# The last feed forward of a decoder: a pipeline over pairs of items, candidates split at the eighth key

## The chip, the cores and the metric

One core of one Trainium2 chip runs the whole kernel in one launch. The metric is the device time of that core in microseconds (us), as the median of several runs; less is better. The engines of a core work side by side and meet only at semaphores: TensorE (PE, with its weight loads PEld), VectorE (DVE), ScalarE (ACT), GpSimd (POOL) and SyncE (SP).

## What is computed

A decoder of four layers on x of 32 items x 128 tokens x 128 features, in float32; each layer has an attention, a cross attention and a feed forward. Only the last of these twelve stages is touched. For each item it computes, of the normalised x (`hidden_states`):

```python
H=4 heads, nk=64 keys, K=8, 512 experts
sim = einsum('pbthn,hkpn->pbthk', q, keys)          # q = hidden_states @ W_q.T, p = x half and y half
scores_xy, idx_xy = top_k(sim, K)                   # the 8 best keys of each half
all_scores = sx[..., :, None] + sy[..., None, :]    # 64 sums per head
all_idx = ix[..., :, None] * nk + iy[..., None, :]
scores, pk = top_k(all_scores, K)                   # the 8 best sums
w = silu(hidden . down_embed[indices] * softmax(scores))
experts_states = sum over h, k of w * up_embed[indices]
dense = silu(hidden @ W_up.T) @ W_down.T
x = x + dense + experts_states
```

There are 512 embeddings, and an index is ix * 64 + iy. So an index whose x key is 8 or more lies past the end and is taken as the last one, 511. Both kernels use this: only the first 8 x keys need a grid of 8 x 64 = 512 weights, one per embedding, and what falls on all other x keys goes to embedding 511.

## The kernel before, in words

Tokens lie on the 128 partitions. The stage is `l3_ffn`, with 32 items in a hardware loop of 16 trips of U = 2 items on each engine (`Fori`, lines 2563, 2630 and 2653). Inside a trip every engine goes through its steps for item 0 and item 1, and each step waits on a semaphore with the item's number. Nothing of the next trip begins before the last step of this one: VectorE's first step (L100, normalise) comes after its last (L2626, x plus result).

The order within a trip, per item:

- VectorE normalises; TensorE transposes (L2656) and ScalarE copies to xT (L2633); TensorE multiplies by W_q (L2660), ScalarE copies to qT (L2636); TensorE multiplies by down_embed (L2663, 128x512, into `p_dot`) and by the keys (L2666, into `p_sim`), then by W_up (L2670).
- VectorE takes the 8 best of each half and head (L2573), finds the places of the x ones (L2576), builds 64 candidate sums per head (L2582) and 512 grid sums per head (L2586), and takes the 8 best candidates (L2593).
- ScalarE takes exp of all 2304 sums (L2639). VectorE zeroes what is under the eighth best (L2599, L2602), adds up and inverts (L2605, L2606), and multiplies by the inverse and by `p_dot` (L2609, L2611). ScalarE takes silu of 2304 (L2645).
- VectorE sums what fell past the eighth key (L2616, L2618, L2620) and adds the four heads (L2622, L2623). TensorE transposes the 512 weights (L2675), ScalarE copies (L2648), TensorE multiplies the dense and the expert parts into `p_dot` (L2681, L2683), VectorE adds to x (L2626).

The helper `skewed` (L180), used by other stages and by the changed one, yields steps t: the step calls `item(lag)` and gets pair t - lag, if there is one. The first steps stand as straight code, then a loop, then straight code again. `Steps` is the `Chain` of the other stages; a chained instruction is waited for on its own engine.

## Time and profile before

| | us |
|---|---|
| median of 3 runs | 6312.41 (6308.8 to 6314.84) |
| the profiled execution, own time | 6316.28 |
| its span | 6314.5 |
| VectorE busy in it | 3620.7 (57%) |
| TensorE busy | 3596.9 (57%) |
| ScalarE busy | 1577.1 (25%) |
| last stage in it, first instruction to last | 5531.2 to 6304.2 |

Reading: the page gives whole-span shares, which mix twelve stages. The last stage is the stretch from 5531 us on, and its rows come from the views by stretch. A row of the groups by line says: line, engine, operation, tiles written <- read, shapes, xcount | busy us, mean ns of one | idle time before it and who ended it. A row of the timeline says: start us, duration, engine, line, operation, xcount, and in brackets the idle time before it and who ended that. Neighbouring instructions on an engine overlap, so the distance between starts can be less than the duration; the chain of work gives that distance. In a row of the windows the stretch and its length come first, then the busy time and count of PE, PEld, DVE, ACT and POOL, then the granted TensorE clock (1.00 is 2.4 GHz, 0.50 is 1.2 GHz), the DMA share and GB/s. A float32 matmul shows as two instructions (x8 is 4 of them).

### The profile page before, as it was taken

What the parts mean: (1) busy time and instruction counts of PE and PEld (TensorE: products, weight loads), DVE (VectorE), ACT (ScalarE), POOL (GpSimd) and SP (SyncE); (2) the same over time, 40 slices, a digit from 0 to 9 for tenths busy, and PEclk for the clock granted to TensorE, in tenths of its full rate; (3) what the DMA queues carried; (4) which work ended last, traced back from release to release, by engine and by line L of the source; (5) the groups of instructions that cost most, each with busy time, mean ns of one, the idle gap of its engine ahead of it and who ended that gap; (6) DMA issues with size and microseconds to landing.
All of it is one profiled execution on the core that took longest, in us unless ns stands there. A gap on an engine that the chain in (4) does not pass through costs nothing. (4 is left out here: it accounts for less than half of the span.)

```text
span 6314.5 us, 71361 instructions
## 1 busy us (share of the span) xinstructions
PE 3596.9 (57%) x21570; PEld 2472.5 (39%) x21634; DVE 3620.7 (57%) x10096; ACT 1577.1 (25%) x3714; POOL 749.3 (12%) x1030
## 2 busy tenths in 40 slices
PE   4679999534346601601533344489978887833333
PEld 4456666312114400501422233356656665523222
DVE  2453333688896530554577755444446665567776
ACT  1452232100004300200111111233324443423332
POOL 0240000000003257075000000000000000000000
PEclk9789999766668755555655556589989999966666
DMA  3000000000000000300200000000000000000000
GB/s 80 4 10 5 10 10 5 8 0 0 0 0 12 16 2 1 84 1 3 59 0 0 0 6 0 7 3 10 7 14 0 0 0 3 0 10 0 0 0 13
DMA packets 84128, 60.48 MB, mean 10 GB/s; under 512 B 21067, under 2 KB 78744, under 8 KB 83332
## 3 DMA queue, kind: packets, MB, share of 16 engines
q1 hardware_dynamic: 67164, 56.87, 3.2%
q0 software_dynamic: 12288, 0.68, 0.2%
q10 hardware_dynamic: 4608, 2.10, 0.1%
q8 instruction: 34, 0.56, 0.0%
q14 instruction: 34, 0.28, 0.0%
HBM read 64.98 MB, written 19.14 MB: 13 GB/s over the span
## 5 line engine op out<-in xcount | busy, mean ns | idle before, releaser
L398 DVE TENSOR_TENSOR l_ffn_h<-l_ffn_sg,l_ffn_p_u 128x512 f32<-128x512 f32 (+1 forms) x448 | 308.0, 688 | 408.2 <-PE l_ffn_p_u L371 406.6
L387 ACT ACTIVATE l_ffn_sg<-l_ffn_p_g 128x512 f32<-128x512 f32 (+1 forms) x448 | 267.5, 597 | 819.0 <-PE l_ffn_p_g L368 805.0
L371 PE MATMUL l_ffn_p_u<-l_ffn_f_xTall,l_ffn_wu 128*128 (+1 forms) x896 | 461.2, 596 | 8.4 <-DVE l_ffn_h L398 8.4
L368 PE MATMUL l_ffn_p_g<-l_ffn_f_xTall,l_ffn_wg 128*128 (+1 forms) x896 | 461.8, 597 | 1.9 <-DVE l_ffn_f_logits L259 1.0
L377 PEld LDWEIGHTS l_ffn_p_o<-l_ffn_wd,l_ffn_h 128*128 128x128 f32 (+1 forms) x3584 | 410.3, 192 | 31.0 <-issue 31.0
L377 PE MATMUL l_ffn_p_o<-l_ffn_wd,l_ffn_h 128*128 128x128 f32 (+1 forms) x3584 | 410.6, 275 | 0.0
L95 POOL TENSOR_TENSOR rstd<-vareps,minus_half 128x32 f32<-128x32 f32 x12 | 65.2, 5435 | 2860.9 <-DVE vareps L86 2134.2
L994 PE MATMUL l_attn_p_s<-l_attn_outer,l_attn_upper 128*128 128x512 f32 x256 | 191.7, 917 | 298.5 <-DVE l_attn_outer L905 232.0
L407 DVE SCALAR_TENSOR_TENSOR x<-l_ffn_p_o,l_ffn_cw,x 128x128 f32 x512 | 171.2, 351 | 284.2 <-PE l_ffn_p_o L377 282.4
L2675 PE MATMUL l_ffn_p_sim<-ident,l_ffn_w 128*128 128x128 f32 x128 | 35.6, 433 | 481.8 <-DVE l_ffn_w L2623 481.8
L371 PEld LDWEIGHTS l_ffn_p_u<-l_ffn_f_xTall,l_ffn_wu 128*128 128x128 f32 (+1 forms) x896 | 166.2, 186 | 230.5 <-issue 221.3
L368 PEld LDWEIGHTS l_ffn_p_g<-l_ffn_f_xTall,l_ffn_wg 128*128 128x128 f32 (+1 forms) x896 | 162.2, 186 | 192.2 <-issue 191.7
L994 PEld LDWEIGHTS l_attn_p_s<-l_attn_outer,l_attn_upper 128*128 128x128 f32 x256 | 73.5, 302 | 412.2 <-issue 331.6
L2281 ACT ACTIVATE l_attn_E<-l_attn_p_s,l_attn_nm 128x128 f32<-128x128 f32 x512 | 182.7, 382 | 156.3 <-DVE l_attn_nm L2244 156.3
L1641 POOL DMA_INDIRECT l_combine_got<-slots_out,l_combine_at x192 | 211.0, 1099 | 60.7 <-issue 49.0
L2675 PEld LDWEIGHTS l_ffn_p_sim<-ident,l_ffn_w 128*128 128x128 f32 x128 | 22.8, 216 | 491.2 <-DVE l_ffn_w L2623 491.2
L1745 PE MATMUL l_attn_p_t<-ident,l_attn_xhat 128*128 128x128 f32 x32 | 9.6, 448 | 340.8 <-DVE l_attn_xhat L100 340.8
L1426 POOL DMA_INDIRECT slots_in<-l_route_xd,l_route_at x192 | 187.3, 975 | 58.1 <-issue 40.5
L1936 PE MATMUL l_film_p_a<-ident,l_film_mean 128*120 128x128 f32 x32 | 15.0, 467 | 306.9 <-DVE l_film_mean L1873 306.9
L371 PE MATMUL l_route_p_u<-l_route_f_xTall,l_route_wu 128*88 x32 | 19.5, 696 | 263.4 <-issue 263.4
L980 ACT ACTIVATE l_attn_st<-l_attn_st 128x32 f32<-128x32 f32 x48 | 11.0, 229 | 603.6 <-DVE l_attn_st L885 333.7
L2301 PEld LDWEIGHTS l_attn_p_y<-l_attn_xT,l_attn_wqkv 128*128 128x128 f32 x1024 | 130.2, 192 | 42.7 <-issue 31.5
(690 smaller groups left out, 8992.1 us busy)
## 6 DMA issues: line engine op xcount, KB each, us to landing
l_attn_toep<-kernel_rows SPq DMA_DIRECT2D x1, 8192.0 KB, 31.5
ssm_toep<-ssm_rows SPq DMA_DIRECT2D x1, 8192.0 KB, 31.4
l_slots_w<-in_L_ffn_w SPq DMA_DIRECT2D x32, 176.0 KB, 2.3
slots_in<-l_route_xd,l_route_at POOLq DMA_INDIRECT x192
l_combine_got<-slots_out,l_combine_at POOLq DMA_INDIRECT x192
l_slots_w<-in_L_ffn_w SPq DMA_DIRECT2D x32, 88.0 KB
x<-in_x SPq DMA_DIRECT2D x1, 2048.0 KB
l_ffn_wg<-in_L_ffn_w_gate SPq DMA_DIRECT2D x8, 256.0 KB, 2.7
```

Source lines behind the costliest of these rows:

```text
L95: pool.tensor_tensor(R.rstd[:], R.vareps[:], R.minus_half[:], ALU.pow).then_inc(s.rstd_ready, 1)
L368: pe.matmul(X.p_g[0:X.FP, k % 2], X.wg[:, w, f * X.FP:(f + 1) * X.FP], x, start=True, stop=True).then_inc(s.gate_psum, 1)
L371: pe.matmul(X.p_u[0:X.FP, k % 2], X.wu[:, w, f * X.FP:(f + 1) * X.FP], x, start=True, stop=True).then_inc(s.up_psum, 1)
L377: mm = pe.matmul(X.p_o[:, v, q * P:(q + 1) * P], X.h[:, v, f, q * P:(q + 1) * P], X.wd[:, w, f * P:(f + 1) * P], start=(f == 0), stop=(f = ...
L387: act.activation(X.sg[:, k % 2], X.p_g[0:X.FP, k % 2], ACT.Silu).then_inc(s.silu_ready, 1)
L398: dve.tensor_tensor(X.h[:, k // X.FC, k % X.FC], X.sg[:, k % 2], X.p_u[0:X.FP, k % 2], ALU.mult).then_inc(s.h_ready, 1)
L407: add = dve.scalar_tensor_tensor(out=row(R.x, b), in0=X.p_o[:, v, q * P:(q + 1) * P], scalar=weight, in1=row(R.x, b), op0=ALU.mult, op1=AL ...
L994: mm = pe.matmul(p_s[:, r, a], upper[:], outer[:, u, r, a * 512:(a + 1) * 512], start=True, stop=True)
L1426: pool.indirect_dma_start(xb, bass.IndirectOffsetOnAxis(ap=at[:, u, k:k + 1], axis=0), xd[:, u], None, bounds_check=last, oob_is_err=False ...
L1641: pool.indirect_dma_start(got[:, u, k], None, yb, bass.IndirectOffsetOnAxis(ap=at[:, u, k:k + 1], axis=0), bounds_check=last, oob_is_err=F ...
L2281: e = act.activation(E[:, u % 2, h], p_s[:, u % 2, odd, c * P:(c + 1) * P], ACT.Exp, bias=nm[:, u % 2, h:h + 1], accum_out=sums[:, u % 2, ...
L2301: mm = pe.matmul(p_y[:, c * P:(c + 1) * P], wqkv[:, w:w + P], xT[:, u // 2], start=True, stop=True)
```

## The change

The stage works on pairs (16) as a pipeline of depth 3: in step t, pair t is normalised and scored (item 0), pair t-1 gets its candidates, sums and exp (item 1), pair t-2 its weights (item 2), and pair t-3 is transposed, multiplied and added to x (item 3). There are 19 steps. The x keys are split at the eighth: the 16 x values per head are the first 8 keys and the 8 best of the other 56, so no place has to be looked up, and `cand` holds 128 sums per head. VectorE multiplies exp by `p_dot` and by the comparison with the eighth best, while the division is left to ScalarE: silu gets the inverse as its per-partition `scale`, one activation per head, and a second, with an accumulator, sums what goes to embedding 511. The four heads are added by TensorE: 16 matmuls with the identity per item, accumulating in PSUM, stand in place of 4 transposes. x comes to the output sum by a matmul with the identity; ScalarE copies the result back over x, and normalises too. Lines that stand for removed or unchanged code are "...".

```diff
@@ -2525,23 +2525,23 @@
...
+    NG_, NC = H * NE, H * 2 * K * K
+    W, PAIRS, PER2 = 2 * P, NB // 2, 2
+    with phase(nc, "l3_ffn", "var_ready rstd_ready shift_ready w_in vchain xhat_ready xT_psum xT_ready q_psum q_ready sim_psum sums_ready cut_ready exp_ready "
+                   "dot_psum w_ready silu_ready rest_added up_psum h_ready wT_psum wT_ready out_psum out_taken") as (s, sb, ps):
...
+        xhat, xT, qT = sb("xhat", [P, W]), sb("xT", [P, PER2, W]), sb("qT", [P, HF, W])
+        top, first, m, xs = sb("top", [P, 2, 2 * H, K]), sb("first", [P, 2 * H]), sb("m", [P, 2 * H]), sb("xs", [P, 2 * H, 2 * K])
+        sums, cand = sb("sums", [P, PER2, 2, NG_]), sb("cand", [P, PER2, 2 * H, 2 * K * K])
+        cut, fit, z = sb("cut", [P, PER2, 2 * H, K]), sb("fit", [P, 2 * H, K * K]), sb("z", [P, 2 * H])
+        w, e_c, e_t = sb("w", [P, PER2, 2, NG_]), sb("e_c", [P, PER2, 2 * H, K * K]), sb("e_t", [P, PER2, 2 * H, K])
+        rz, rest, spare = sb("rz", [P, PER2, 2 * H]), sb("rest", [P, PER2, 2 * H]), sb("spare", [P, K * K])
+        hT, wT = sb("hT", [P, PER2, HF, W]), sb("wT", [P, 2, HF, P])
+        p_q, p_sim, p_dot = ps("p_q", [P, HF, W]), ps("p_sim", [P, 2, 512]), ps("p_dot", [P, 2, 512])
+        p_w, p_x = ps("p_w", [P, 512]), ps("p_x", [P, 2, W])
...
@@ -2554,134 +2554,160 @@
...
+                chain = Steps(dve, s.vchain)
...
+                def added(b, u, r):
+                    dve.wait_ge(s.silu_ready, b * 2 + (r + 1))
+                    last = w[:, u, r].rearrange("p (h k) -> p h k", h=H)[:, :, NE - 1]
+                    dve.tensor_tensor(last, last, rest[:, u, r * H:(r + 1) * H], ALU.add).then_inc(s.rest_added, 1)
+                for item in skewed(dve, 3, PAIRS, PER2):
...
+                    for b, u in item(3):
+                        added(b, u, 0)
+                    for b, u in item(1):
+                        sim = p_sim[:].rearrange("p r (a h k) -> p r a h k", a=2, h=H)
+                        dve.wait_ge(s.sim_psum, b * 2 + 2)
+                        dve.tensor_reduce(first[:].rearrange("p (r h) -> p r h", r=2), sim[:, :, 0, :, 0:K], AX.X, ALU.max)
+                        for r in range(2):
...
+                                dve.max(top[:, 0, r * H + h], sim[:, r, 0, h, K:NK])
+                                last = dve.max(top[:, 1, r * H + h], sim[:, r, 1, h])
...
+                        chain(dve.tensor_tensor(m[:], first[:], top[:, 0, :, 0], ALU.max))
+                        chain(dve.tensor_tensor(m[:], m[:], top[:, 1, :, 0], ALU.add))
+                        dve.tensor_tensor(xs[:, :, 0:K].rearrange("p (r h) k -> p r h k", r=2), sim[:, :, 0, :, 0:K],
+                                          m[:].rearrange("p (r h) -> p r h", r=2).unsqueeze(3).broadcast_to((P, 2, H, K)), ALU.subtract)
+                        chain(dve.tensor_tensor(xs[:, :, K:2 * K], top[:, 0], m[:].unsqueeze(2).broadcast_to((P, 2 * H, K)), ALU.subtract))
+                        chain(dve.tensor_tensor(cand[:, u].rearrange("p g (i j) -> p g i j", i=2 * K),
+                                                xs[:].unsqueeze(3).broadcast_to((P, 2 * H, 2 * K, K)),
+                                                top[:, 1].unsqueeze(2).broadcast_to((P, 2 * H, 2 * K, K)), ALU.add))
+                        for g in range(2 * H):
+                            last = dve.max(cut[:, u, g], cand[:, u, g])
+                        last.then_inc(s.cut_ready, 1)
+                    for b, u in item(3):
+                        added(b, u, 1)
+                    for b, u in item(1):
+                        for r in range(2):
+                            dve.tensor_tensor(sums[:, u, r].rearrange("p (h i j) -> p h i j", h=H, i=K),
+                                              xs[:, r * H:(r + 1) * H, 0:K].unsqueeze(3).broadcast_to((P, H, K, NK)),
+                                              sim[:, r, 1].unsqueeze(2).broadcast_to((P, H, K, NK)), ALU.add).then_inc(s.sums_ready, 1)
+                    for b, u in item(2):
+                        dve.wait_ge(s.exp_ready, b + 1)
+                        chain(dve.tensor_reduce(z[:], e_t[:, u], AX.X, ALU.add))
+                        dve.reciprocal(rz[:, u], z[:])
+                        chain(dve.tensor_tensor(fit[:], cand[:, u, :, K * K:2 * K * K], cut[:, u, :, K - 1:K].broadcast_to((P, 2 * H, K * K)), ALU.is_ge))
+                        for r in range(2):
+                            dve.wait_ge(s.dot_psum, b * 2 + (r + 1))
+                            chain(dve.tensor_tensor(w[:, u, r].rearrange("p (h k) -> p h k", h=H), w[:, u, r].rearrange("p (h k) -> p h k", h=H),
+                                                    p_dot[:, r].unsqueeze(1).broadcast_to((P, H, NE)), ALU.mult))
+                            g = slice(r * H, (r + 1) * H)
+                            dve.scalar_tensor_tensor(out=e_c[:, u, g].rearrange("p g k -> p (g k)"), in0=e_c[:, u, g].rearrange("p g k -> p (g k)"),
+                                                     scalar=p_dot[:, r, NE - 1:NE], in1=fit[:, g].rearrange("p g k -> p (g k)"), op0=ALU.mult, op1=ALU.mult)
+                            for h in range(H):
+                                n = slice(h * NE, (h + 1) * NE)
+                                last = dve.scalar_tensor_tensor(out=w[:, u, r, n], in0=sums[:, u, r, n], scalar=cut[:, u, r * H + h, K - 1:K],
+                                                                in1=w[:, u, r, n], op0=ALU.is_ge, op1=ALU.mult)
+                            last.then_inc(s.w_ready, 1)
...
+                def silus(b, u, r):
+                    act.wait_ge(s.w_ready, b * 2 + (r + 1))
+                    for h in range(H):
+                        n, g = slice(h * NE, (h + 1) * NE), r * H + h
+                        act.activation(w[:, u, r, n], w[:, u, r, n], ACT.Silu, scale=rz[:, u, g:g + 1])
+                        last = act.activation(e_c[:, u, g], e_c[:, u, g], ACT.Silu, scale=rz[:, u, g:g + 1], accum_out=rest[:, u, g:g + 1])
+                    last.then_inc(s.silu_ready, 1)
+                act.wait_ge(s.shift_ready, 1)
+                for item in skewed(act, 3, PAIRS, PER2):
+                    for b, u in item(3):
+                        silus(b, u, 1)
+                    for b, u in item(2):
+                        act.wait_ge(s.up_psum, b + 1)
+                        act.activation(hT[:, u].rearrange("p c t -> p (c t)"), p_q[:].rearrange("p c t -> p (c t)"), ACT.Silu).then_inc(s.h_ready, 1)
+                    for b, u in item(0):
+                        for r in range(2):
+                            last = act.activation(xhat[:, r * P:(r + 1) * P], row(R.x, b * 2 + r), ACT.Identity,
+                                                  scale=R.rstd[:, bass.ds(b * 2 + r, 1)], bias=R.shift[:, bass.ds(b * 2 + r, 1)])
+                        last.then_inc(s.xhat_ready, 1)
+                    for b, u in item(3):
+                        for r in range(2):
+                            act.wait_ge(s.wT_psum, b * 2 + (r + 1))
+                            act.activation(wT[:, r].rearrange("p c t -> p (c t)"), p_w[:], ACT.Copy).then_inc(s.wT_ready, 1)
+                        act.wait_ge(s.out_psum, b + 1)
+                        act.activation(pair(R.x, b), side(p_x[:, 1]), ACT.Copy).then_inc(s.out_taken, 1)
+                    for b, u in item(0):
+                        act.wait_ge(s.xT_psum, b + 1)
+                        act.activation(xT[:, u], p_x[:, 0], ACT.Copy).then_inc(s.xT_ready, 1)
+                        act.wait_ge(s.q_psum, b + 1)
+                        act.activation(qT[:].rearrange("p c t -> p (c t)"), p_q[:].rearrange("p c t -> p (c t)"), ACT.Copy).then_inc(s.q_ready, 1)
+                    for b, u in item(1):
+                        act.wait_ge(s.cut_ready, b + 1)
+                        act.activation(e_c[:, u], cand[:, u, :, K * K:2 * K * K], ACT.Exp)
+                        act.activation(e_t[:, u].rearrange("p g k -> p (g k)"), cut[:, u].rearrange("p g k -> p (g k)"), ACT.Exp)
+                        for r in range(2):
+                            act.wait_ge(s.sums_ready, b * 2 + (r + 1))
+                            last = act.activation(w[:, u, r], sums[:, u, r], ACT.Exp)
+                        last.then_inc(s.exp_ready, 1)
+                    for b, u in item(2):
+                        silus(b, u, 0)
...
+                for item in skewed(pe, 3, PAIRS, PER2):
+                    for b, u in item(2):
+                        for r in range(2):
+                            after(pe, s.w_ready, b * 2 + (r - 1))
+                            pe.matmul(p_dot[:, r], xT[:, u, r * P:(r + 1) * P], down[:], start=True, stop=True).then_inc(s.dot_psum, 1)
+                        for c, _ in item(1):
+                            pe.wait_ge(s.q_ready, c + 1)
...
+                            mm = pe.matmul(p_q[:, c], wup[:, c * P:(c + 1) * P], xT[:, u], start=True, stop=True)
+                        mm.then_inc(s.up_psum, 1)
+                    for b, u in item(3):
+                        for r in range(2):
+                            pe.wait_ge(s.rest_added, b * 2 + (r + 1))
+                            after(pe, s.wT_ready, b * 2 + r)
+                            for c in range(HF):
+                                for h in range(H):
+                                    n = h * NE + c * P
+                                    mm = pe.matmul(p_w[:, c * P:(c + 1) * P], w[:, u, r, n:n + P], R.ident[:], start=(h == 0), stop=(h == H - 1))
+                            mm.then_inc(s.wT_psum, 1)
+                        pe.wait_ge(s.h_ready, b + 1)
+                        for c, _ in item(1):
+                            pe.wait_ge(s.xT_ready, c + 1)
+                        for r in range(2):
+                            o = p_x[:, 1, r * P:(r + 1) * P]
+                            pe.matmul(o, R.ident[:], row(R.x, b * 2 + r), start=True, stop=False)
+                            for c in range(HF):
+                                pe.matmul(o, hT[:, u, c, r * P:(r + 1) * P], wdn[:, c], start=False, stop=False)
+                            pe.wait_ge(s.wT_ready, b * 2 + (r + 1))
+                            for c in range(HF):
+                                mm = pe.matmul(o, wT[:, r, c], up[:, c], start=False, stop=(c == HF - 1))
+                        mm.then_inc(s.out_psum, 1)
+                    for b, u in item(0):
+                        pe.wait_ge(s.xhat_ready, b + 1)
+                        for c, _ in item(3):
+                            pe.wait_ge(s.out_taken, c + 1)
+                        for r in range(2):
+                            mm = pe.transpose(p_x[:, 0, r * P:(r + 1) * P], xhat[:, r * P:(r + 1) * P], R.ident[:])
+                        mm.then_inc(s.xT_psum, 1)
+                        pe.wait_ge(s.xT_ready, b + 1)
+                        for c, _ in item(2):
+                            pe.wait_ge(s.h_ready, c + 1)
+                        for c in range(HF):
+                            mm = pe.matmul(p_q[:, c], wq[:, c * P:(c + 1) * P], xT[:, u], start=True, stop=True)
...
+                        pe.wait_ge(s.q_ready, b + 1)
+                        for r in range(2):
+                            after(pe, s.sums_ready, b * 2 + (r - 1))
+                            for c in range(HF):
+                                mm = pe.matmul(p_sim[:, r, c * P:(c + 1) * P], qT[:, c, r * P:(r + 1) * P], keys[:, c], start=True, stop=True)
+                            mm.then_inc(s.sim_psum, 1)
...
```

## Rows read from the trace of the kernel before

**Rows 1.** The page: the chain that ended last, share by engine.

```profile
DVE 9%; PE 3%; issue 0%; DVEq 0%; POOLq 0%; ACT 0%
```

**Rows 2.** Windows: busy PE, PEld, DVE, ACT, POOL; PEclk, DMA. A trip, half.

```profile
5589.00:5637.00 48.00, 16.08 (x96) 13.92 (x96) 34.99 (x117) 15.08 (x15) 0.00 (x0) 0.64 0.00 0
5884.00:5910.00 26.00, 0.00 (x0) 0.00 (x0) 25.32 (x83) 10.02 (x7) 0.00 (x0) 0.54 0.00 0
```

**Rows 3.** Chain in order of time (start, us): one point of two trips.

```profile
5876.11 2.05 PE l_ffn_p_x L2660 x16
5893.34 0.66 DVE l_ffn_w L2602
5923.89 2.05 PE l_ffn_p_x L2660 x16
```

**Rows 4.** Groups by line, last stage: busy us, mean ns, idle before, releaser.

```profile
L2602 DVE SCALAR_TENSOR_TENSOR l_ffn_w<-l_ffn_sums,l_ffn_cut,l_ffn_w 128x512 f32<-128x512 f32 x128 | 95.4, 745 | 0.0
L2611 DVE SCALAR_TENSOR_TENSOR l_ffn_w<-l_ffn_w,l_ffn_z,l_ffn_p_dot 128x512 f32<-128x512 f32 x128 | 94.8, 740 | 0.0
L2586 DVE TENSOR_TENSOR l_ffn_sums<-l_ffn_gridx,l_ffn_p_sim 128x512 f32<-128x512 f32 x128 | 86.8, 678 | 0.0
L2645 ACT ACTIVATE l_ffn_w<-l_ffn_w 128x2304 f32<-128x2304 f32 x32 | 67.9, 2123 | 155.9 <-DVE l_ffn_w L2611 155.9
L2622 DVE TENSOR_TENSOR l_ffn_w<-l_ffn_w 128x1024 f32<-128x1024 f32 x32 | 39.2, 1225 | 1.1
L2675 PE MATMUL l_ffn_p_sim<-ident,l_ffn_w 128*128 128x128 f32 x128 | 35.6, 433 | 481.8 <-DVE l_ffn_w L2623 481.8
L2648 ACT ACTIVATE l_ffn_wT<-l_ffn_p_sim 128x512 f32<-128x512 f32 x32 | 19.1, 597 | 70.2 <-PE l_ffn_p_sim L2675 70.2
```

**Rows 5.** Groups by line, whole kernel: wide VectorE forms elsewhere.

```profile
L1348 DVE TENSOR_TENSOR l_combine_terms<-l_combine_fine,l_combine_coarse 128x2048 f32<-128x2048 f32 x8 | 18.3, 2292 | 0.0
L915 DVE TENSOR_REDUCE l_attn_step<-l_attn_part 128x256 f32<-128x2048 f32 x32 | 122.5, 3828 | 1.1
```

**Rows 6.** Timeline (start, us): ScalarE with per-partition operand and accumulator.

```profile
5001.15 0.36 ACT L2281 ACTIVATE l_attn_E<-l_attn_p_s,l_attn_nm 128x128 f32<-128x128 f32 x1
5001.40 0.20 ACT L2281 ACTIVATION_READ_ACCUMULATOR l_attn_E<-l_attn_p_s,l_attn_nm 128x1 f32 x1
5001.50 0.36 ACT L2281 ACTIVATE l_attn_E<-l_attn_p_s,l_attn_nm 128x128 f32<-128x128 f32 x1
```

**Rows 7.** Timeline, last stage: transposes, matmuls and maxima in a row.

```profile
5875.41 0.59 PE L2656 MATMUL l_ffn_p_x<-ident,l_ffn_xhat 128*128 128x128 f32 x2 [1.68 <-DVE l_ffn_xhat L100]
5878.86 1.05 PE L2666 MATMUL l_ffn_p_sim<-l_ffn_keys,l_ffn_qT 128*128 128x128 f32 x8
5880.18 1.15 DVE L2573 MAX8 l_ffn_top<-l_ffn_p_sim 128x8 f32<-128x64 f32 x8
```

**Rows 8.** Timeline and groups by line: table loads.

```profile
5894.47 1.28 ACT L2642 ACT_TABLE_LOAD   x1
5895.77 1.09 ACT L2642 ACTIVATE l_ffn_hT<-l_ffn_p_x 128x512 f32<-128x512 f32 x2
L387 ACT ACT_TABLE_LOAD x68 | 87.2, 1283 | 1.2
```

**Rows 9.** Timeline and windows around a PE pause, and after a trip.

```profile
3015.64 1.20 PE L1745 MATMUL l_attn_p_t<-ident,l_attn_xhat 128*128 128x128 f32 x4 [5.00 <-DVE l_attn_xhat L100]
3014.00:3015.00 1.00, 0.00 (x0) 0.00 (x0) 0.19 (x2) 0.00 (x0) 0.00 (x0) 1.00 0.00 0
3016.00:3017.00 1.00, 1.00 (x5) 0.50 (x4) 0.10 (x1) 0.51 (x2) 0.00 (x0) 0.50 0.00 0
5886.00:5888.00 2.00, 0.00 (x0) 0.00 (x0) 1.81 (x14) 1.86 (x1) 0.00 (x0) 0.52 0.00 0
```

**Rows 10.** Timeline: first and last VectorE steps of the stage.

```profile
5545.78 0.19 DVE L2570 COPY l_ffn_gridx<-l_ffn_p_sim 128x32 f32<-128x32 f32 x1 [7.08 <-PE l_ffn_p_sim L2666]
6303.93 0.29 DVE L2626 TENSOR_TENSOR x<-x,l_ffn_p_dot 128x128 f32 x1 [2.10 <-PE l_ffn_p_dot L2683]
```

123 lines of the change are left out of this document (removed).

## The prediction

> **What bounds the kernel now.** The chain that ended last [rows 1] gives VectorE 9% and TensorE 3% of the span and ScalarE next to nothing: its traced part lies in the last stage, so this stage is serial, and VectorE is most of it. One fixed point of a trip comes back after 5923.89 - 5876.11 = 47.78 us [rows 3]; 16 such trips make the stage. In 48 us VectorE is busy 35.0, TensorE 16.1, ScalarE 15.1 [rows 2], and in the second half of a trip TensorE does nothing for 26 us while VectorE is busy 25.3 [rows 2]. TensorE's 481.8 us before L2675 [rows 4] are this wait. So a trip is 35 us of VectorE and about 13 us in which VectorE waits for the others. Two things can be won: VectorE's work, and that 13 us. Nothing outside the stage changes, so I count only from 5531 to 6304 us of the profiled execution.
>
> **Prices.** VectorE, f32: 1225 ns for 1024 elements against 678 for 512 [rows 4], so 1.07 ns per element; 2.29 us for 2048 [rows 5]; 0.66 us from start to start for a 128x512 with a per-partition scalar [rows 3]; 8 maxima over 64 in 1.15 us [rows 7], so 0.144 each, and about 0.21 over 128; small steps 0.2 [rows 10]. ScalarE: (2123 - 597) / (2304 - 512) = 0.85 ns per element [rows 4], so 0.38 us for 256, 1.03 for 1024, 1.9 for 2048. A 128x128 with a per-partition operand and an accumulator, its reading included, repeats every 0.35 us [rows 6]; with 64 elements that is 0.30, and without the reading but with 512 elements 0.58. No row shows a silu with a per-partition scale; without one, two of 512 follow each other in 1.09 [rows 8], so 0.49 apart, and a full duration with the operand's 0.09 would be 0.69. I take 0.58, from rows 6; the ends are 0.4 us less or more per four. A table load is 1.28 [rows 8]. TensorE at 2.4 GHz: 8 instructions, 4 matmuls of 128 columns, in 1.05 less a tail of 0.2 [rows 7], so 0.213 per matmul; 256 columns twice that, 512 four times. Adding heads is such matmuls with a new weight load for each; in a trip the loads' 13.9 us lie beside the matmuls' 16.1 [rows 2], so I price them as matmuls alone. If no load were hidden the heads of an item would take 3.4 us more.
>
> **VectorE after, per pair.** Removed are the look-up of places, the grid by single heads, the second multiplication (L2611, 94.8 us in all), the sum over heads (L2622 alone 39.2) [rows 4]. What is left, in the order of a step: rest added twice 0.3; candidates: a reduction 0.2, 16 maxima 2.3, two small steps 0.35, two more 0.4, 1024 sums 1.25, 8 maxima over 128 1.7, together 6.2; the two grids 2 x 2.2 = 4.4; sum, inverse, comparison 1.1; per item 2.3 (2048 times p_dot) + 0.35 + 4 x 0.66 = 5.3, twice 10.6. With 0.5 for the loop and the chain's reset that is 23.1 us against 35.
>
> **ScalarE after, per pair.** Two times four silus of 512 and of 64: 4 x (0.58 + 0.30) + 0.1 = 3.6, twice 7.2; hT 1.03; normalise 2 x 0.3; wT 2 x 0.6; x 0.4; xT 0.4; qT 1.03; exp of candidates, cuts and two grids 0.5 + 0.1 + 1.75 + 1.9 = 4.2; two loads 2.6. About 18.7 us. The loads stay two, since the steps before the loop leave silu's table in place as the loop does; a loop that had to reload at its head would look like L387, 68 loads [rows 8], and cost 1.28 in every second step.
>
> **TensorE after, per pair.** dot 2 x 0.85, up 1.7, 32 matmuls that add heads 6.8, out 18 x 0.213 = 3.85, transposes 0.3, queries 1.7, sim 1.7: 17.8 us at 2.4 GHz, 35.6 at 1.2.
>
> **The ring.** Each engine has a fixed order, so the step is not the busiest engine but the longest ring through the orders. I follow one step from the moment a at which ScalarE ends item 2's first silus, the last thing in its step:
> - VectorE adds the rest of the first item (0.2), then does all candidate work of the next pair (6.2), and only then adds the rest of the second item (0.2). ScalarE finished that item's silus at a + 3.6, so this wait is by order alone: a + 6.6.
> - TensorE adds the heads of the second item, 16 x 0.213 = 3.4, and the outputs of both, for which ScalarE's copy is ready in time, 3.85, tail and hand-off 0.25: a + 14.1. Queued behind on ScalarE, which waits for this, are the copy to x, item 0's copies, all exps and the next silus.
> - ScalarE copies to x, 0.45: a + 14.55. TensorE may only now transpose, 0.5 (0.59 for two with a wait between [rows 7]); ScalarE copies xT, 0.45; TensorE's queries, 1.95; ScalarE's qT, 1.05: a + 18.5.
> - ScalarE loads exp (1.3), does the exps (4.2), loads silu (1.3) and does the silus (3.6): a + 28.9.
>
> VectorE ends its step at a + 23, before the next a; TensorE's dots and up follow at once and end by a + 25.6; sim of the next pair ends at a + 20.3. All three are hidden, by ScalarE's exps and silus; without that cover the 2.6 of dot and up would come in. The first item's heads (a + 0.3 to a + 3.7) lie beside VectorE's candidates. So the ring is 28.9 us, with VectorE idle for nearly 6 of them.
>
> **The clock.** TensorE is busy 17.8 of 28.9 us, with a pause of 3.7 us before the heads of the first item and of 2.8 before those of the second. After a pause of 5.0 us the clock was still 1.00 in its last whole us and 0.50 soon after work began again; after a trip, with nothing from 5884 on [rows 2], it was down at 5886 [rows 9]. So 3.7 us can go either way. If the first item's heads run at 1.2 GHz they take 6.8 and end 0.6 late; the rise may fall into the second's, and the queries cost 1.7 more if the clock fell before them. Bounds: 0 and 4.4 us per step. I take 1.1, nearer to nothing, since TensorE works in every quarter of the step: 30.0 us.
>
> **A rule weighed.** The load at 5894.47 takes 1.28 us and the activation follows at 5895.77 [rows 8], so nothing but the load stands between. The Trainium skill (ScalarE: Activation LUTs, "What ACT_TABLE_LOAD costs") adds a drain of about 1.4 us to each switch; by it, as an estimate, both loads would lengthen the ring by some 2.8 us and the stage by about 36. The trace does not show it, and my sum is without it.
>
> **The sum.** Start: VectorE's first step of scoring is at 5545.8 before [rows 10], after 0.6 us more TensorE work at 5546.4. Then candidates and grids of pair 0 (10.6), a wait of 1.6 for the scores of pair 1, since `p_sim` has one buffer, 10.6 again, and the weights of pair 0, 11.7: at 5580.9 the first full ring begins. 13 rings of 30.0: 5970.9. The step without item 0 saves transposes, xT, queries and qT, 24.9. In the next VectorE goes on at once, 3.8 + 11.7 = 15.5; the last is silus 3.6, rest 0.2, heads and outputs 7.5, copy 0.5. That is 27.3, so the end is 6023.1, against 6304.2 before [rows 10]: 281 us less. 6316.3 - 281 = 6035 for the profiled execution; the median is 3.9 below that execution, which gives 6031.
>
> **Rivals.**
> - *The order does not bind, VectorE does.* If the ring is shorter than I read it, VectorE's 23.1 is the floor: 13 x 6.9 = 90 us less, 5941. For it: VectorE is the busiest engine. Against: the waits as the code has them. Chance 0.12 for 23.1 to 28.5 us per step (5941 to 6012).
> - *The clock stays low.* The heads, outputs, transposes and queries of the ring double: 9.3 more per step, less the 1.1 counted, plus some 5 at the ends: 13 x 8.2 + 5 = 112, 6143. For it: TensorE pauses in each step; before, trips start at 1.2 GHz each time. Against: at half speed it would be busy almost without a break, and no pause reaches 5.0. The Trainium skill (TensorE: Matmul & The Clock Gate, "HAM oscillation — how this bites in real kernels") tells of a kernel whose every tile starts cold after a wait, which is this case. Chance 0.10 for 32.5 to 38 us per step (6064 to 6143).
> - *The pipeline does not overlap.* If VectorE's whole step lies in the ring, 23.1 in place of 6.6, a step is 46.5 and the time 6031 + 13 x 16.5 = 6245. It needs item 2's weights to wait for something of this step's end; they wait for the exp of the step before. Chance 0.03. A lesser case, loads at each loop head or dearer activations, gives 31.5 to 32.5 (up to 6064) and is in the forecast.
> - *Slower: wide forms with broadcast operands run at a fraction of the rate.* A reduction of 2048 took 3.83 us where another form takes 2.29 [rows 5]. The two grids, two p_dot products, the 1024 sums and the comparison are 10.7 us of VectorE's step. At 3.83 / 2.29 they add 7 and VectorE stands at 30, hardly over the ring. Only from a step of some 50 us, where they cost over 3.5 times my price, is the kernel slower than before, at 6320 and more. Against: L2586 has both broadcasts at the normal rate [rows 4]. Chance 0.02.
>
> **Chances.** Forecast 0.73 (28.5 to 32.5 us per step, 6012 to 6064). I let the range run from 5985 to 6100, which takes in half of each neighbour and leaves about 0.15 out. A change under 0.2% (12.6 us) is about what cannot be told from none here. Faster by more 0.97, within 0.01, slower by more 0.02.
>
> **What the changed trace would show.** The distance of one fixed point in two steps, 29 to 31 us. VectorE's rows near 23 us per step, and its idle time before the first rest added, released by ScalarE's silu. ScalarE idle before the second wT copy, before the copy to x and before qT, all released by TensorE. TensorE idle before the second item's heads, released by VectorE's small addition. Granted clock over 0.85. Two loads per step. It would be wrong if VectorE's idle time is near zero, if ScalarE's small activations with an accumulator cost much more than 0.30, or if the clock is near 0.6.

## The result, and the profile after

The changed kernel takes 6055.75 us (median of four executions, 6044.85 to 6058.01) against 6313.62 for the kernel before beside it: a ratio of 0.9589, 95% interval 0.9572 to 0.9605. Predicted were 6031, with 5985 to 6100. The direction and the cause held; the gain was 8% smaller than forecast. Run a second time, unedited, the changed kernel took 6047.18 against 6316.57 (0.9575, interval 0.9559 to 0.9591).

The page of the changed kernel: the chain that ended last, by engine. In [rows 1] VectorE stood first with 9%.

```profile
PE 4%; ACT 3%; DVE 1%; issue 1%; DMA 0%; SPq 0%; ACTq 0%
```

VectorE has dropped to 1% of the chain and TensorE and ScalarE share the rest: the chain now goes through a ring of three engines, each for part of a step.

Windows of the changed kernel, columns as in [rows 2]: nine steps together, then three stretches of 2 us around the start of one step's heads.

```profile
5660.00:5930.00 270.00, 193.37 (x1204) 168.84 (x1203) 193.49 (x431) 171.78 (x339) 0.00 (x0) 0.89 0.00 0
5799.00:5801.00 2.00, 0.00 (x0) 0.00 (x0) 0.00 (x0) 2.00 (x7) 0.00 (x0) 1.00 0.00 0
5801.00:5803.00 2.00, 0.04 (x1) 0.04 (x1) 0.26 (x2) 2.00 (x7) 0.00 (x0) 0.60 0.00 0
5803.00:5805.00 2.00, 2.00 (x9) 2.00 (x10) 2.00 (x17) 2.00 (x7) 0.00 (x0) 0.50 0.00 0
```

In 270 us TensorE and VectorE are each busy 193, ScalarE 172. In a trip of [rows 2] it was 16, 35 and 15 of 48. So all three engines work 64 to 72% of the time, and none of them is the bound by itself.

The timeline of the changed kernel over one steady step, VectorE, TensorE and ScalarE in turn (start, duration, engine, line, tiles, count, idle time before it and who ended that):

```profile
5802.74 0.17 DVE L2563 TENSOR_TENSOR l_ffn_w<-l_ffn_w,l_ffn_rest 128x4 f32<-128x4 f32 x1 [8.18 <-ACT l_ffn_e_c L2621]
5808.79 0.15 DVE L2563 TENSOR_TENSOR l_ffn_w<-l_ffn_w,l_ffn_rest 128x4 f32<-128x4 f32 x1
5822.50 2.74 DVE L2610 SCALAR_TENSOR_TENSOR l_ffn_w<-l_ffn_sums,l_ffn_cut,l_ffn_w 128x512 f32<-128x512 f32 x4
5833.50 0.17 DVE L2563 TENSOR_TENSOR l_ffn_w<-l_ffn_w,l_ffn_rest 128x4 f32<-128x4 f32 x1 [8.26 <-ACT l_ffn_e_c L2621]
...
5802.96 6.33 PE L2678 MATMUL l_ffn_p_w<-ident,l_ffn_w 128*128 128x128 f32 x32 [5.49 <-DVE l_ffn_w L2563]
5810.07 3.81 PE L2678 MATMUL l_ffn_p_w<-ident,l_ffn_w 128*128 128x128 f32 x32 [0.78 <-ACT l_ffn_wT L2639]
...
5818.04 0.39 ACT L2641 ACTIVATE x<-l_ffn_p_x 128x256 f32 x1 [3.52 <-PE l_ffn_p_x L2690]
5821.55 1.02 ACT L2646 ACTIVATE l_ffn_qT<-l_ffn_p_q 128x1024 f32<-128x1024 f32 x1 [2.15 <-PE l_ffn_p_q L2703]
5822.59 1.28 ACT L2649 ACT_TABLE_LOAD   x1
5823.89 0.63 ACT L2649 ACTIVATE l_ffn_e_c<-l_ffn_cand 128x512 f32<-128x512 f32 x1
5828.29 1.28 ACT L2620 ACT_TABLE_LOAD   x1
5829.58 0.72 ACT L2620 ACTIVATE l_ffn_w<-l_ffn_w,l_ffn_rz 128x512 f32<-128x512 f32 x1
```

Read it as the ring. VectorE begins a step at 5802.74 after 8.18 us of idling that ScalarE's last silu ends, and the next at 5833.50: 30.76 us, where a trip of [rows 3] took 47.78. TensorE's first heads take 6.33 us, the same 32 instructions at 5810.07 only 3.81: the first run at 1.2 GHz for most of their time (granted clock 0.50), after a pause of 5.49. ScalarE then waits 3.52 for the outputs, 2.15 for the queries, and from 5822.59 on works without a gap to the end of the ring. VectorE has ended its step at 5825.2 and has nothing to do.

The stage, from its first weight transfer to its last copy to x, takes 511.3 us (5535.45 to 6046.7) against 773.0 (5531.23 to 6304.2): 261.7 us less, against 258 by the medians. Most of the difference between the two is that the stage began 4.2 us later in this execution.

### The profile page after: what moved, and what is told of

The parts are those of the page before. It is cut to its first block and busy times, and to the rows that moved or that the text cites. A ratio compares the mean times of both kernels' runs of the same rounds, so it can differ in the third digit from the quotient of the medians.

```text
span 6056.1 us, 72210 instructions
## 1 busy us (share of the span) xinstructions
PE 3717.2 (61%) x22338; PEld 2565.9 (42%) x22338; DVE 3417.2 (56%) x9024; ACT 1643.8 (27%) x4097; POOL 749.3 (12%) x1030
## 5 line engine op out<-in xcount | busy, mean ns | idle before, releaser
L2678 PE MATMUL l_ffn_p_w<-ident,l_ffn_w 128*128 128x128 f32 x1024 | 155.2, 323 | 87.0 <-DVE l_ffn_w L2563 74.9
L2678 PEld LDWEIGHTS l_ffn_p_w<-ident,l_ffn_w 128*128 128x128 f32 x1024 | 150.0, 236 | 95.3 <-DVE l_ffn_w L2563 83.3
```

The costliest lines, as they stand in the source:

```text
L2678: mm = pe.matmul(p_w[:, c * P:(c + 1) * P], w[:, u, r, n:n + P], R.ident[:], start=(h == 0), stop=(h == H - 1))
```

## The experiments

Each is one edit of the changed kernel. The kernel of e2 adds work whose result nobody reads, as do those of e1 and e8. In the profiled executions the stage starts anywhere from 5515.9 us (e8) to 5538.7 (e10), so the whole time can move by more than most of these edits change it, and the stage's length and the distance of the first small additions (the step) are compared as well. "Stage" and "step" below are read from each kernel's timeline that way; the step is the mean over the steady part. Which steps are taken for steady moves that mean by up to 0.1 us, so a difference of 0.1 says nothing.

| kernel | ratio to before [95%] | stage, us | step, us | granted clock | VectorE busy of 270 us |
|---|---|---|---|---|---|
| changed | 0.9589 [0.9572, 0.9605] | 511.3 | 30.6 | 0.89 | 193 |
| e9 no overlap | 1.0002 [0.9992, 1.0011] | 772.0 | 47.9 | 0.74 | 122 |
| e2 more VectorE work | 0.9608 [0.9592, 0.9624] | 520.1 | 30.7 | 0.90 | 234 |
| e1 pause filled | 0.9591 [0.9575, 0.9607] | 519.4 | 30.8 | 0.96 | 193 |
| e8 both pauses filled | 0.9577 [0.9561, 0.9593] | 512.6 | 29.7 | 1.00 | 199 |
| e3 small additions first | 0.9577 [0.9561, 0.9593] | 505.3 | 29.8 | 0.90 | 201 |
| e4 heads on VectorE | 0.9624 [0.9608, 0.9640] | 532.3 | 32.4 | 0.76 | 217 |
| e6 division on VectorE | 0.9553 [0.9537, 0.9569] | 490.7 | 29.0 | 0.91 | 222 |
| e5 exps moved | 0.9452 [0.9436, 0.9467] | 430.3 | 24.0 | 0.98 | 247 |
| e7 e5 and e6 | 0.9447 [0.9432, 0.9463] | 430.7 | 23.9 | 0.98 | 263 |
| e10 e5, half of e6 | 0.9451 [0.9435, 0.9466] | 424.1 | 23.6 | 0.99 | 259 |

**Is the gain overlap, or VectorE's lighter work?** e9 keeps every operation and takes the overlap away. Beside the lines shown, the steps of each engine are put in the order of a single pair. The last line is the one copy that it adds.

```diff
-                for item in skewed(dve, 3, PAIRS, PER2):
+                for item in serial(dve):          # every item(lag) is the same pair; ScalarE and TensorE likewise
...
+                        act.activation(spare[:, u:u + 1], p_x[:, 1, 0:1], ACT.Copy)
```

> All the changed kernel's operations in their new forms, but every engine does a pair's whole work before it takes the next: no overlap between pairs. (One ScalarE copy of one column is added per pair.) Theory that the gain comes from the overlap: a pair's own chain is then what the whole stage is made of, VectorE's 22.3 us and about as much on ScalarE and TensorE that lies between them; I put it at 48 us, about what a trip of the kernel before took (47.78), so the stage is 16 x 48 + 12 = 780 us and the kernel about 6320, the same as before. Rival, that the gain comes from the 13 us of VectorE's work taken away per trip, with overlap or without: a step of 35 us and a kernel of about 6110.

Measured: 6316.51 us against 6316.57, a step of 47.9 and a stage of 772.0. In its windows (a pair is 48 us) and its timeline:

```profile
5697.00:5745.00 48.00, 22.57 (x138) 19.24 (x138) 22.51 (x50) 19.88 (x39) 0.00 (x0) 0.75 0.00 0
...
5705.81 0.22 DVE L2598 TENSOR_REDUCE l_ffn_z<-l_ffn_e_t 128x8 f32<-128x64 f32 x1 [1.98 <-ACT l_ffn_w L2646]
5721.74 0.17 DVE L2567 TENSOR_TENSOR l_ffn_w<-l_ffn_w,l_ffn_rest 128x4 f32<-128x4 f32 x1 [3.88 <-ACT l_ffn_e_c L2625]
5741.15 0.22 DVE L2574 TENSOR_REDUCE l_ffn_first<-l_ffn_p_sim 128x8 f32<-128x64 f32 x1 [19.24 <-PE l_ffn_p_sim L2682]
```

VectorE's 22.5 us and three waits of 1.98, 3.88 and 19.24 us make the pair. VectorE had 35 us and some 13 of waiting [rows 2]; now it has 22.5 and 25. The new forms alone win nothing: the work that they take off VectorE comes back on TensorE and ScalarE (16.1 and 15.1 us in [rows 2], 22.6 and 19.9 here) in series. The whole gain needs the pipeline. That the two times agree to 0.1 us is luck: another order within the pair could move e9 somewhat, and none was tried. The rival, 6110 us from the lighter work alone, falls.

**Is VectorE off the ring?** e2 adds 4.6 us of VectorE work between the grids of one pair and the weights of the other.

```diff
+                        for _ in range(2):
+                            chain(dve.tensor_tensor(extra[:], sums[:, u, 0], sums[:, u, 1], ALU.add))
```

> Two additions of 2048 elements that nobody reads are added to VectorE's step after the grids, some 4.6 us. If VectorE binds, the step goes from 30.5 to 35 and the kernel to about 6116. Ring theory: VectorE has 8.2 us idle per step, so the work is hidden; and since the dot of the second item and W_up now end 4 us later, TensorE's pause before the heads shrinks to about 1 us, the clock stays up and the step falls to 29.3 us, the kernel to about 6040. If the ring holds but the clock costs nothing: 6056.

Measured: VectorE's work rose from 193 to 234 us in 270, the step from 30.6 to 30.7. The whole time is 6061 and the ratio 0.0019 above the changed kernel's, hardly outside either interval. VectorE is not the bound, as the 8.2 us of idling said: bound by it, the step would be 35.

The expected 29.3 us and 6040 failed, though. The mean of 30.7 is made of steps of 29.6 us, shorter than any steady step of the changed kernel, and of steps of 31.0 to 31.3. TensorE's timeline of e2 shows one cause of the long ones:

```profile
5766.61 2.08 PE L2668 MATMUL l_ffn_p_dot<-l_ffn_down,l_ffn_xT 128*128 128x512 f32 x2 [3.85 <-DVE l_ffn_w L2613]
```

VectorE's extra work puts off the second dot, TensorE pauses before it, and in some steps dot and W_up then run at 1.2 GHz and hold up the heads. In other steps the second heads take 5.4 to 5.5 us, as in e1 below. So the 4.6 us are not simply hidden: what the first heads gain is lost again by the clock in two steps of three.

The stage grew by 9 us, nearly all of it where the ring is not full: the first ring begins 56.2 us into the stage instead of 51.9, and the last step but one takes 21.3 us instead of 17.3. There VectorE's work is in the sum, as the prediction had it.

**What does the clock cost?** e1 gives TensorE work in the pause before the first heads, e8 in the one before the second too.

```diff
+                        for _ in range(4):                                  # e1 and e8, after W_up
+                            pe.matmul(p_w[:], R.ident[:], down[:], start=True, stop=True)
...
+                                for _ in range(5):                          # e8 only, after the first heads
+                                    pe.matmul(p_x[:, 0], R.ident[:], down[:, 0:W], start=True, stop=True)
```

> Four matmuls of 512 columns into p_w, which nobody reads, are added after the multiplication by W_up; they fill 3.4 of the 5.5 us for which TensorE pauses before the first item's heads. Clock theory: the granted clock stays at 1.00 through the step, the first item's heads take 3.6 us instead of 6.3, the second's begin 6.2 us after the first small addition instead of 7.4 (VectorE's order then decides), the step goes from 30.5 to 29.3 us, and the kernel from 6056 to about 6038. Rival, the clock costs nothing because the first item's heads are hidden anyway: 6056. Rival, TensorE's own work binds: 3.4 us more per step, 6100.

Measured: 30.8 us per step, no gain; the expectation of 29.3 failed. TensorE's timeline of e1, two steps:

```profile
5777.83 3.84 PE L2680 MATMUL l_ffn_p_w<-ident,l_ffn_w 128*128 128x128 f32 x32 [2.08 <-DVE l_ffn_w L2563]
5783.87 3.84 PE L2680 MATMUL l_ffn_p_w<-ident,l_ffn_w 128*128 128x128 f32 x32 [2.20 <-DVE l_ffn_w L2563]
...
5807.47 3.84 PE L2680 MATMUL l_ffn_p_w<-ident,l_ffn_w 128*128 128x128 f32 x32 [1.04 <-DVE l_ffn_w L2563]
5813.50 5.47 PE L2680 MATMUL l_ffn_p_w<-ident,l_ffn_w 128*128 128x128 f32 x32 [2.19 <-DVE l_ffn_w L2563]
```

The first heads now run at the high clock (3.84), and for that very reason end early: TensorE waits 2.2 us for VectorE's second addition, after that pause the clock is low in two steps of three, and the second heads take 5.4 to 5.5. The second heads begin 6.25 us after the first small addition, 1.1 earlier than in the changed kernel, as expected; but they lie in the ring whole, and 1.6 us more in two steps of three is as much on average. The slow first heads had been covering a pause.

> With the first filling alone the clock fell in the 2.2 us pause between the two items' heads in two of three steps, and the second heads (in the ring) took 5.5 us in place of 3.8; its fast steps took 29.6 us. Here five matmuls of 256 columns into the unused half of p_x fill that pause as well. Clock theory: every step takes 29.3 to 29.7 us, granted clock 1.00, kernel about 6042, so the clock's price in the changed kernel is 0.9 to 1.2 us per step, close to the 1.1 of the prediction. If the clock still falls, it is not the pauses of the heads that decide, and the step stays above 30.

Measured: granted clock 1.00, step 29.7 (the first three 36.5, 31.0 and 31.0), as expected, so the low clock costs the changed kernel about 1.0 us a step. The prediction's bounds were 0 and 4.4, its value 1.1. As a repair it is worthless: the filling makes the first steps longer, and the stage is 512.6 us.

**Does the order on VectorE cost 6 us?** e3 puts both small additions ahead of the candidates.

```diff
                     for b, u in item(3):
                         added(b, u, 0)
+                        added(b, u, 1)
...
-                    for b, u in item(3):
-                        added(b, u, 1)
```

> VectorE adds the rest of the second item directly after that of the first, before the candidates of the next pair. Ring theory: it then waits 3.6 us for the second silus, which costs nothing out of its idle 8.2; the second item's heads can start 4.7 us after the first small addition instead of 7.4; w_ready and with it TensorE's dot come 3.6 us later, so the pause is short and the clock stays up; the step falls from 30.5 to 27.9 us and the kernel to about 6022. If only the clock matters and not the order of the small addition: 29.3 us and 6040. If VectorE binds, its new wait of 3.6 us costs in full: 6103.

Measured: 6043.23 us, step 29.8, where 27.9 were expected. The timeline of e3 shows what came instead, in two steps:

```profile
5759.90 0.87 ACT L2632 ACTIVATE l_ffn_xhat<-x,shift,rstd 128x128 f32 x2
5760.67 0.58 ACT L2638 ACTIVATE l_ffn_wT<-l_ffn_p_w 128x512 f32<-128x512 f32 x1
5761.39 3.81 PE L2677 MATMUL l_ffn_p_w<-ident,l_ffn_w 128*128 128x128 f32 x32 [1.15 <-ACT l_ffn_wT L2638]
...
5781.57 2.08 PE L2664 MATMUL l_ffn_p_dot<-l_ffn_down,l_ffn_xT 128*128 128x512 f32 x2 [4.25 <-DVE l_ffn_w L2609]
5783.44 3.38 PE L2668 MATMUL l_ffn_p_q<-l_ffn_xT,l_ffn_wup 128*128 128x256 f32 x8
5784.74 0.17 DVE L2563 TENSOR_TENSOR l_ffn_w<-l_ffn_w,l_ffn_rest 128x4 f32<-128x4 f32 x1 [3.22 <-ACT l_ffn_e_c L2620]
5786.66 3.73 PE L2677 MATMUL l_ffn_p_w<-ident,l_ffn_w 128*128 128x128 f32 x32
5788.52 0.17 DVE L2563 TENSOR_TENSOR l_ffn_w<-l_ffn_w,l_ffn_rest 128x4 f32<-128x4 f32 x1 [3.61 <-ACT l_ffn_e_c L2620]
```

In the first one, whose first small addition is at a = 5755.35, the first heads are done in time, and TensorE waits 1.15 us more for ScalarE's copy of them. ScalarE comes to that copy only at a + 5.3: it works without a gap through the second silus, hT and the normalising. So the second heads can't begin before a + 6.04, where the expectation had a + 4.7. It had left out ScalarE's order, and that is 1.3 of the 1.9 us missing a step.

In the second one, a = 5784.74, something else comes on top. VectorE's addition ends at 5784.9, but the heads start at 5786.66: they are queued behind the second dot and W_up. These waited 4.25 us for the end of VectorE's step and then ran at 1.2 GHz (2.08 us; 1.05 for the same two instructions at 5805.69). The second heads begin at a + 6.4 for it; over the steady steps it is a + 6.3 on average. In the prediction dot and W_up were "hidden, by ScalarE's exps and silus"; here they are not always, since VectorE stands 3.61 us at the second addition before it may begin the candidates, and so ends its step later.

**The heads on TensorE.** e4 adds them on VectorE again, as the kernel before did, and transposes the sum.

```diff
+                    chain(dve.tensor_tensor(w[:, u, r, 0:2 * NE], w[:, u, r, 0:2 * NE], w[:, u, r, 2 * NE:4 * NE], ALU.add))
+                    dve.tensor_tensor(w[:, u, r, 0:NE], w[:, u, r, 0:NE], w[:, u, r, NE:2 * NE], ALU.add).then_inc(s.rest_added, 1)
...
-                                    mm = pe.matmul(p_w[:, c * P:(c + 1) * P], w[:, u, r, n:n + P], R.ident[:], start=(h == 0), stop=(h == H - 1))
+                                mm = pe.transpose(p_w[:, c * P:(c + 1) * P], w[:, u, r, c * P:(c + 1) * P], R.ident[:])
```

> One part undone: VectorE adds the four heads again (2048 elements in two additions per item, some 3.9 us per pair), and TensorE transposes 4 times in place of 16 matmuls. If adding heads on TensorE is itself a gain, the kernel is slower by VectorE's 3.9 us per step: 6107. Ring theory: 3.9 us come in on VectorE's side of the ring (1.95 before the candidates, 1.95 after) and 2.9 to 3.0 go on TensorE's, with 1.2 of waiting for the first item's heads, so at an unchanged clock the step stays at 30.5 within 0.5; but TensorE is busy only 12 us of it and the outputs and queries may run at 1.2 GHz, which costs up to 5.7 us. 6055 to 6125, with the granted clock of the outputs telling which.

Measured: 6074.43 us, step 32.4, inside the range given. TensorE's timeline of e4, of one step:

```profile
5759.45 1.11 PE L2678 MATMUL l_ffn_p_w<-ident,l_ffn_w 128*128 128x128 f32 x4 [6.85 <-DVE l_ffn_w L2565]
5760.78 1.91 PE L2687 MATMUL l_ffn_p_x<-l_ffn_wdn,l_ffn_hT 128*128 128x128 f32 x8
```

The transposes are short, but TensorE comes to them from a pause of 6.85 us and does the first outputs at 1.2 GHz: eight instructions in 1.91 us, where the last eight, at 5765.64, take 1.06. Adding the heads on TensorE is worth about 1.8 us a step, 21 us of the stage, what it does to the clock included.

**The exps out of the ring.** The ring has 4.4 us of exps and a table load that wait for nothing in it: their operands are ready when VectorE is done with candidates and sums. e5 puts them between the two copies of item 3's heads, where ScalarE waits for TensorE.

```diff
+                    for r in range(2):
                         for b, u in item(3):
-                        for r in range(2):
                             act.wait_ge(s.wT_psum, b * 2 + (r + 1))
                             act.activation(wT[:, r]..., p_w[:], ACT.Copy).then_inc(s.wT_ready, 1)
+                        for b, u in item(1):
+                            if r == 0: ...                                  # cut_ready; exp of e_c and of e_t
+                            act.wait_ge(s.sums_ready, b * 2 + (r + 1))
+                            last = act.activation(w[:, u, r], sums[:, u, r], ACT.Exp)
```

> ScalarE's exps of the next pair move from behind item 0's copies to between the copies of item 3: exp of candidates, cuts and the first grid after the first wT copy, exp of the second grid after the second. They then lie in the 4 us and 3.5 us for which ScalarE waits for TensorE. Ring theory: exp load and exps leave the ring (6.1 us off, about 1.3 us of the second one's wait comes back nowhere), one table load stays: queries end at a + 17.2, qT 18.2, load 19.5, silus 23.4. VectorE's own step is 22.4, TensorE's work 17.8. The step falls from 30.5 to between 23.5 and 25 us, up to 26.5 where TensorE runs at 1.2 GHz; stage 85 us shorter, kernel about 5968 (5950 to 6000). Rival, ScalarE's order does not matter since VectorE or TensorE binds: 6056.

Measured: 5966.8 us, 1.5% less than the changed kernel, step 24.0, as expected. The timeline of e5:

```profile
5760.98 1.28 ACT L2645 ACT_TABLE_LOAD   x1 [0.30 <-DVE l_ffn_cut L2587]
5763.19 1.92 ACT L2648 ACTIVATE l_ffn_w<-l_ffn_sums 128x2048 f32<-128x2048 f32 x1
5765.01 0.58 ACT L2639 ACTIVATE l_ffn_wT<-l_ffn_p_w 128x512 f32<-128x512 f32 x1
5772.53 1.02 ACT L2658 ACTIVATE l_ffn_qT<-l_ffn_p_q 128x1024 f32<-128x1024 f32 x1 [2.15 <-PE l_ffn_p_q L2707]
5773.57 1.28 ACT L2620 ACT_TABLE_LOAD   x1
5778.78 0.17 DVE L2563 TENSOR_TENSOR l_ffn_w<-l_ffn_w,l_ffn_rest 128x4 f32<-128x4 f32 x1 [1.52 <-ACT l_ffn_e_c L2621]
```

After qT comes only the load of silu's table, not the exps. VectorE's idle time fell from 8.2 to 1.5 us, and the heads are at the high clock (3.73 at 5756.06 and 3.84 at 5761.02). Removed from the ring are one load (1.3), the exps (4.4) and the slow clock (1.0): 6.7 us, against a difference of 6.6 between 30.6 and 24.0. This is the sharpest test of the ring, and it holds.

**The division.** e6 gives it back to VectorE: per item one silu of 2048 and one of 256 instead of four of 512 and four of 64.

```diff
-                            chain(dve.tensor_tensor(w[:, u, r]..., w[:, u, r]..., p_dot[:, r]...broadcast_to((P, H, NE)), ALU.mult))
+                            for h in range(H):
+                                last = dve.scalar_tensor_tensor(out=w[:, u, r, n], in0=w[:, u, r, n], scalar=rz[:, u, r * H + h:r * H + h + 1], in1=p_dot[:, r], op0=ALU.mult, op1=ALU.mult)
...
-                        act.activation(w[:, u, r, n], w[:, u, r, n], ACT.Silu, scale=rz[:, u, g:g + 1])
-                        last = act.activation(e_c[:, u, g], e_c[:, u, g], ACT.Silu, scale=rz[:, u, g:g + 1], accum_out=rest[:, u, g:g + 1])
+                    act.activation(w[:, u, r], w[:, u, r], ACT.Silu)
+                    act.activation(g, g, ACT.Silu, accum_out=rest[:, u, r:r + 1]).then_inc(s.silu_ready, 1)
```

> One part undone: the division goes back to VectorE (p_dot product and inverse in one instruction per head, 4 x 0.66 in place of 2.3 us per item, and one product of the comparison with the inverse, 0.7 per pair), and ScalarE takes one silu of 2048 and one of 256 per item, 2.4 us in place of 3.8. If leaving the division to ScalarE's scale is a gain, the kernel gets slower by VectorE's 1.4 us per step, 6074. Ring theory: VectorE's 1.4 us is hidden in its idle 8.2, ScalarE's 1.45 us comes off the ring once per step: 29.1 us, and 27.9 if the shorter pause keeps the clock up: kernel 6022 to 6040.

Measured: 6029.45 us, step 29.0, as expected. This part of the change lost time: 1.6 us a step, 20 us in the stage. ScalarE's silus of an item take 2.2 us instead of 3.8, and they are in the ring, while VectorE has 8 us to spare.

e7 is the edits of e5 and e6 together. e10 is e5 with the candidates' part of e6 alone:

```diff
+                        chain(dve.tensor_tensor(fit[:], fit[:], rz[:, u].unsqueeze(2).broadcast_to((P, 2 * H, K * K)), ALU.mult))
...
-                        last = act.activation(e_c[:, u, g], e_c[:, u, g], ACT.Silu, scale=rz[:, u, g:g + 1], accum_out=rest[:, u, g:g + 1])
+                    act.activation(g, g, ACT.Silu, accum_out=rest[:, u, r:r + 1]).then_inc(s.silu_ready, 1)
```

> Both edits before together. The ring would be 23.4 - 1.45 = 22.0 us, below VectorE's step of 22.4 + 1.4 = 23.8, so now VectorE binds: its idle time nearly vanishes, 24 us per step, kernel about 5965, the same as with the exps moved alone within 10 us. If the ring still decides: 22.5 per step and 5945.

> The kernel with the exps moved between item 3's wT copies (e5), in which only the candidates' part of the division returns to VectorE: its product costs VectorE 0.64 us per pair, and each item's four silus of 64 with a scale become one silu of 256, 0.8 us less per item on ScalarE. If ScalarE's silus are in the ring, as I think, the step falls from 24.0 to about 23.3 us and the kernel takes about 5957. If VectorE, 91% busy in e5, is what binds by then, the step stays at 24.0 and the kernel at about 5967.

Measured: e7 5962.04 us with a step of 23.9, e10 5971.3 with 23.6. Expected was that VectorE binds in e7 and that e10 wins 0.7 us a step; it won 0.4, and its whole time is 5971 for the expected 5957. The windows of e5, e7 and e10:

```profile
5660.00:5930.00 270.00, 218.07 (x1526) 188.31 (x1524) 246.62 (x541) 212.43 (x424) 0.00 (x0) 0.98 0.00 0
5660.00:5930.00 270.00, 217.92 (x1530) 188.70 (x1530) 262.92 (x606) 177.17 (x215) 0.00 (x0) 0.98 0.00 0
5660.00:5930.00 270.00, 218.28 (x1526) 187.70 (x1526) 258.77 (x562) 197.92 (x295) 0.00 (x0) 0.99 0.00 0
```

VectorE is busy 91, 97 and 96% (third busy column). At 97% it is the bound, and the ratios of the three cannot be told apart. So this line of repair ends at VectorE's work, 23.3 us a pair in e7 (262.92 / 270 x 23.9). All three beat both kernels, by 1.4 to 1.5% and by 5.5%.

The changed kernel, unedited, ran once more beside e9 and e10.

> The changed kernel once more, unedited, beside the other two on one chip: a step of 30.6 us and a ratio to the kernel before within 0.0015 of 0.9589.

Measured: 0.9575 and a step of 30.7, a stage of 511.8 us. The ratio lies 0.0014 below the first one, so a difference of this size between two kernels is not an effect.

## Why the prediction was right, and by how much it was off

The ring, term by term, over the step from a = 5802.74:

| point of the ring | predicted | measured |
|---|---|---|
| VectorE's second small addition ends | a + 6.6 | a + 6.2 |
| second heads begin | a + 6.6 | a + 7.3 |
| outputs ended, copy to x begins | a + 14.1 | a + 15.3 |
| qT ended | a + 18.5 | a + 19.8 |
| load and exps ended | a + 24.0 | a + 25.5 |
| load ended, silus begin | a + 25.3 | a + 26.8 |
| silus ended, next addition | a + 28.9 | a + 30.8 |
| the same with the clock's 1.1 | 30.0 | 30.8 |

- *The order of waits was right at all points but one.* VectorE idles before the first addition, released by ScalarE's silu. ScalarE waits before the copy to x and before qT, released by TensorE. VectorE's step came out at 22.5 us (5802.74 to 5825.24) for 23.1 predicted, so the wide broadcast forms ran at the normal rate (2284 ns for 2048 elements, 2292 in [rows 5]), and the rival that rested on them had no ground. The one exception: TensorE's second heads wait for ScalarE's copy of the first, not for VectorE's second addition, because the first heads ran at the low clock.
- *The clock was rightly sized, in part by luck.* 1.1 predicted, 1.0 by e8, granted clock 0.89 where over 0.85 was forecast. But 1.1 was a choice between bounds of 0 and 4.4, not a sum. The prediction let slow first heads end 0.6 us late and looked for the rest in the second heads and the queries; neither ran slow in the steady steps. What makes the 1.1 is that ScalarE's copy of the first heads, which it had not counted there, comes after them: they end at a + 6.55 and the second begin 0.78 later. The pause before the first heads is 5.5 us, not 3.7: W_up ended where I had it (5797.5, a + 25.4 of the step before, for a + 25.6), but the ring went on 1.8 us longer. The clock was low for the first heads in all twelve ordinary steps after the first ring. Of the rival "the clock stays low" this much came true and no more. The Trainium skill (TensorE: Matmul & The Clock Gate, "HAM oscillation — how this bites in real kernels") describes the tile that starts cold after a wait; 3.81 and 6.33 us for the same 32 instructions are this case's numbers for it. The prediction's reading for that rival, "trips start at 1.2 GHz each time", was wrong: a trip's first 16 instructions of L2660 take 2.05 us [rows 3], the fast rate of [rows 7], and the stretch from 5884 on is the middle of a trip, not its end. What starts at 1.2 GHz there are the transposes and outputs at its end, after 28 us without TensorE work.
- *ScalarE's silus were mis-sized.* A silu of 512 and one of 64 were priced "0.58 + 0.30", 0.88 together; the pair repeats every 0.94 us (timeline below). Over four pairs that is 0.25 us. Two other sizes were off by more and nearly cancel: from the second heads to the copy to x it took 8.0 us for 7.5, and the candidates and the second addition 6.2 for 6.6. With 0.2 more for loads and exps and 0.1 for the way to qT it makes about the 0.53 us per ordinary step. That it is no more owes something to this cancelling.

ScalarE's timeline of the changed kernel, and groups by line of its last stage (busy us, mean ns, idle before, releaser):

```profile
5799.79 0.70 ACT L2620 ACTIVATE l_ffn_w<-l_ffn_w,l_ffn_rz 128x512 f32<-128x512 f32 x1
5800.40 0.33 ACT L2621 ACTIVATE l_ffn_e_c<-l_ffn_e_c,l_ffn_rz 128x64 f32<-128x64 f32 x1
5800.64 0.19 ACT L2621 ACTIVATION_READ_ACCUMULATOR l_ffn_e_c<-l_ffn_e_c,l_ffn_rz 128x1 f32 x1
5800.73 0.71 ACT L2620 ACTIVATE l_ffn_w<-l_ffn_w,l_ffn_rz 128x512 f32<-128x512 f32 x1
...
L2620 ACT ACTIVATE l_ffn_w<-l_ffn_w,l_ffn_rz 128x512 f32<-128x512 f32 x128 | 90.6, 708 | 0.9 <-DVE l_ffn_w L2610 0.7
L2603 DVE TENSOR_TENSOR l_ffn_w<-l_ffn_w,l_ffn_p_dot 128x2048 f32<-128x2048 f32 x32 | 73.1, 2284 | 1.7
L2649 ACT ACT_TABLE_LOAD x15 | 19.2, 1283 | 0.3
L2639 ACT ACTIVATE l_ffn_wT<-l_ffn_p_w 128x512 f32<-128x512 f32 x32 | 19.1, 597 | 82.6 <-PE l_ffn_p_w L2678 82.5
```

- *The loads.* They stand twice a step, 1283 ns each, and the activation starts where the load ends (5828.29 + 1.28 = 5829.57, 5829.58). No drain stands between, nor before: the rule that was weighed (the Trainium skill, ScalarE: Activation LUTs, "What ACT_TABLE_LOAD costs") would have added an estimated 36 us to the stage, more than the whole miss.
- *Where the miss lies.* The profiled execution's stage is 511.3 us where the sum gave 491.9: 19.4 too few. They are the start before the first full ring (51.9 for 49.7, 2.2), the first ring (33.4 for 30.0, 3.4), twelve rings of 30.53 for 30.0 (6.3), the step without item 0 (26.5 for 24.9, 1.6) and the last two (33.2 for 27.3, 5.9). So two thirds of it is outside the ordinary step. (The medians miss by 24.7; the rest is a stage that began 4.2 us later, less 0.9 us after its end, and how the executions scatter.) The prediction reckoned TensorE's clock for the steady step only, and at the ends dot and W_up are not hidden. The timeline of the changed kernel, TensorE in the first ring and the last step, and ScalarE and VectorE in the last step but one:

```profile
5587.48 2.08 PE L2665 MATMUL l_ffn_p_dot<-l_ffn_down,l_ffn_xT 128*128 128x512 f32 x2 [4.08 <-DVE l_ffn_w L2610]
5589.35 3.62 PE L2669 MATMUL l_ffn_p_q<-l_ffn_xT,l_ffn_wup 128*128 128x256 f32 x8
5592.76 3.94 PE L2678 MATMUL l_ffn_p_w<-ident,l_ffn_w 128*128 128x128 f32 x32
...
6031.10 6.60 PE L2678 MATMUL l_ffn_p_w<-ident,l_ffn_w 128*128 128x128 f32 x32 [4.44 <-DVE l_ffn_w L2563]
6038.47 3.81 PE L2678 MATMUL l_ffn_p_w<-ident,l_ffn_w 128*128 128x128 f32 x32 [0.78 <-ACT l_ffn_wT L2639]
...
6026.69 0.38 ACT L2641 ACTIVATE x<-l_ffn_p_x 128x256 f32<-128x256 f32 x1 [3.42 <-PE l_ffn_p_x L2690]
6030.88 0.17 DVE L2563 TENSOR_TENSOR l_ffn_w<-l_ffn_w,l_ffn_rest 128x4 f32<-128x4 f32 x1 [1.59 <-ACT l_ffn_e_c L2621]
```

  The first small addition stood at 5587.35, but the heads start only at 5592.76, behind 5.3 us of dot and W_up at 1.2 GHz. In the last step the first heads take 6.60 us, with nothing beside them to hide it, and the second begin 7.6 us after the first small addition, where the sum had 3.8. The last step but one takes 17.3 us for 15.5, and there it is the term "VectorE goes on at once, 3.8 + 11.7" that failed: VectorE did go on at once, but ScalarE may start the last silus only behind the copy to x, which waits 3.42 us for TensorE, and VectorE then idles 1.59. The 24.9 for the step without item 0 was 28.9 less 4.0, so the clock's 1.1 was left out of it without a reason; the first heads ran slow there too (6.34). Of the start's 2.2, 2.0 lie before VectorE's first scoring.
- The other rivals: VectorE bound only once the exps and the division had left the ring (e7), at 23.9 us a step, near its 23.1. The pipeline does overlap; e9 shows what it would have been without.

## What to carry to other kernels

When work is taken off one engine in a chain that is serial, price the sum of all engines in one trip, not that engine: here 12.5 us less on VectorE came back as as much more of waiting, and only overlap made it a gain (e9). In a pipeline over a fixed order per engine, write the ring down with its waits and then ask which of its operations wait for nothing in it; moving those to where their engine waits anyway was worth another third of the gain (e5, 6.6 us a step). Before moving anything, follow every engine's order anew: e3 was forecast without ScalarE's, and more than half of its gain did not come. Price the first and last rounds by themselves: there the cover is missing and TensorE's clock is low.

## What the runs showed of the hardware

- The clock can be low after a pause of 2.2 us, where [rows 9] has one of 5.0: in e1 the second heads took 5.47 and 5.37 us after a pause of 2.19, but 3.84 after one of 2.20 in another step. What decides between these was not separated.
- The clock can fall inside a pause or just after it. In the changed kernel the pause lasts from 5797.5 to 5802.96; the granted clock is 1.00 up to 5801 and 0.60 from 5801 to 5803, with 0.04 us of work in that stretch, so it fell before the heads began. In [rows 9] it went from 1.00 to 0.52 at 5886 with no work at all. In e1 it is 1.00 in the pause before 5813.50 and 0.50 from 5814 on, with the heads already running.
- A silu with a per-partition scale on 512 elements takes 708 ns, where a copy of that size takes 597. The reading of the accumulator costs 0.09 us from start to start (5800.64 to 5800.73), not the 0.19 that its row shows.
